# A post-norm decoder layer in three-stage software pipeline: scores of two pairs in one visit, over three banks, and new lists for all engines

## The reference, cut to what matters

```
scores = einsum('bqgre,bkge->bgrqk', q, k) / sqrt(64)      # 16 heads of queries, 8 of keys
probs  = softmax(where(causal_mask, -1e6, scores))
z      = einsum('bgrqk,bkge->bqgre', probs, v)
x = layernorm(x + z @ W_out + b_out)
x = layernorm(x + cross_attention(layernorm_affine(x), ctx, top 5 allowed rows))
x = layernorm(x + (silu(x @ wg.T) * (x @ wu.T)) @ wd.T)
```

## Time and profile before

| | |
|---|---|
| median of 3 runs | 2152.0 us (2150.78 to 2153.03) |
| profiled execution | 2153.04 us, its span 2150.9 us |
| PE / PEld busy | 2081.0 us (97%) / 1857.7 us (86%) |
| DVE / ACT / POOL busy | 1574.1 (73%) / 1328.4 (62%) / 387.2 us (18%) |
| mean granted clock of PE | 0.989 |
| chain that ended last | PE 95% |
| DMA | 38.47 MB, 18 GB/s |

### The profile page before, as it was taken

The page is one execution under the profiler, slowest core; times in us unless marked ns, Lnnn a source line. Parts: engine busy times, 40 slices in busy tenths (PEclk is TensorE's granted clock), DMA queues, the critical chain, the costliest instruction groups (busy, mean ns, idle before and its releaser), DMA issues.

```text
span 2150.9 us, 56003 instructions
## 1 busy us (share of the span) xinstructions
PE 2081.0 (97%) x18368; PEld 1857.7 (86%) x18368; DVE 1574.1 (73%) x5700; ACT 1328.4 (62%) x3990; POOL 387.2 (18%) x630
## 2 busy tenths in 40 slices
PE   4899999999999999999999999999999999999986
PEld 3688988898988998988998988988888988888975
DVE  3477777777777777777777777777777777777764
ACT  4666666666666666666666666666666656666642
POOL 3201111111111111111111112111212111211111
PEclk9899999999999999999999999999999999999998
DMA  4100000000000000000000000000000000000000
GB/s 135 41 14 11 10 18 18 18 18 10 13 13 18 18 18 10 17 9 18 18 18 10 18 8 18 18 18 10 18 8 18 18 18 10 18 8 18 14 6 11
DMA packets 48599, 38.47 MB, mean 18 GB/s; under 512 B 19504, under 2 KB 46512, under 8 KB 48560
## 3 DMA queue, kind: packets, MB, share of 16 engines
q1 hardware_dynamic: 48560, 37.96, 6.3%
HBM read 29.56 MB, written 8.39 MB: 18 GB/s over the span
## 4 chain that ended last, share of the span: by engine, by line
PE 95%; ACT 1%; DVE 1%; DMA 1%; POOL 1%; issue 1%; SPq 0%; POOLq 0%; DVEq 0%; ACTq 0%
PE gen L375 19%; PE gen L377 18%; PE gen L376 18%; PE s_ps L509 10%; PE z_ps L543 6%; PE pt_ps L522 3%; PE gen L470 3%; PE gen L457 3%; PE gen L466 3%; PE z_ps L545 3%; PE pt_ps L523 3%; PE pt_ps L527 3%; PE gen L439 3%; PE gen L481 1%; PE gen L434 1%
## 5 line engine op out<-in xcount | busy, mean ns | idle before, releaser
L679 ACT ACTIVATE SM<-SM,least 128x128 f32<-128x128 f32 (+1 forms) x1024 | 454.1, 449 | 88.4 <-DVE least L975 88.3
L975 DVE CUSTOM_DVE_ANT_0 SM<-s_ps,causal 128x128 f32<-128x128 f32 (+1 forms) x1024 | 311.1, 354 | 157.0 <-PE s_ps L509 99.3
L615 ACT ACTIVATE PT<-pt_ps 128x512 f32<-128x512 f32 (+1 forms) x512 | 245.3, 486 | 153.6 <-PE z_ps L545 91.9
L988 DVE TENSOR_SCALAR SM<-SM,total 128x128 f32<-128x128 f32 (+1 forms) x1024 | 290.2, 347 | 9.1
L509 PE MATMUL s_ps<-KT,QT 64*128 64x128 f32 (+1 forms) x2048 | 237.1, 350 | 6.4 <-ACT KT L615 6.4
L662 ACT ACTIVATE G<-gen 128x256 f32<-128x256 f32 x192 | 73.5, 383 | 245.4 <-PE gen L377 243.3
L1133 POOL TENSOR_TENSOR var<-moments,eps 128x2 f32<-128x2 f32 x96 | 18.7, 195 | 1055.1 <-DVE moments L847 1055.1
L679 ACT ACTIVATION_READ_ACCUMULATOR SM<-SM,least 128x1 f32 x1024 | 197.7, 193 | 0.0
L1157 POOL TENSOR_TENSOR H_lo<-G,H_hi 128x256 fp32r<-128x256 f32 x192 | 141.0, 747 | 293.0 <-ACT H_hi L615 292.9
L509 PEld LDWEIGHTS s_ps<-KT,QT 64*128 64x128 f32 x2048 | 135.4, 188 | 45.4 <-issue 23.4
L543 PE MATMUL z_ps<-PT,Vt 128*64 128x256 f32 x1024 | 170.0, 402 | 2.8 <-ACT PT L615 2.7
(11 more groups left out here) (176 smaller groups left out, 6583.9 us busy)
## 6 DMA issues: line engine op xcount, KB each, us to landing
xT_in<-in_xT SPq DMA_DIRECT2D x32, 256.0 KB, 2.8
x_in<-in_x SPq DMA_DIRECT2D x32, 256.0 KB, 2.8
out<-XN SPq DMA_DIRECT2D x32, 256.0 KB, 2.2
ctx_in<-in_ctxT SPq DMA_DIRECT2D x32, 77.0 KB, 2.4
mask_in<-in_maskT SPq DMA_DIRECT2D x32, 77.0 KB, 2.6
QX<-in_wq SPq DMA_DIRECT2D x1, 512.0 KB, 3.7
QP<-in_wq SPq DMA_DIRECT2D x1, 512.0 KB, 5.5
xwk<-in_xwkv SPq DMA_DIRECT2D x1, 512.0 KB, 5.5
```

The costliest lines, as they stand in the source:

```text
L615: return act.activation(o, i, ACT.Copy)
L679: ins = act.activation(part, part, ACT.Exp, scale=-1.0, bias=least[:, i % 2, n:n + 1], accum_out=total[:, i % 2, n:n + 1])
L975: ins = dve.tensor_tensor_reduce(SM[:, i % 2, at:at + keys], s_ps[h][:, t * P:t * P + keys], causal[:, S - keys:S], -SCALE, -3 * NEG, ALU. ...
L988: ins = dve.tensor_scalar(part, part, total[:, i % 2, n:n + 1], None, ALU.mult)
```

## The change

1. `scores(j)` now makes two pairs, 2j and 2j+1, in one visit: eight matmuls (16 records), four visits an iteration. There are three score banks. The 128-key parts of head 0 and head 1 of both pairs go to banks 0 and 1, as do the 256-key parts of the first pair; both 256-key parts of the second pair go to bank 2. Since head 0 and head 1 run on different array rows, the last matmul waits until the first is through (`s_shared`). DVE's `masked` waits for the whole visit.
2. `BANKS` is 2: two general banks are left.
3. `SM`, `least`, `total` have four places, and `masked(i)` waits for the transposes of pair i-4.
4. The lists of all four engines and `ITEMS` are new. Nothing is computed in another way, and no instruction is added but for the waits.

```diff
-BANKS = 3
+BANKS = 2
+    PLACES = (((0, S), (1, S)), ((0, S + P), (1, S + P))), (((0, 0), (1, 0)), ((2, 0), (2, S)))
-        SM = sb("SM", [P, 2, PAIR])
+        SM = sb("SM", [P, 4, PAIR])
-        s_ps = [bank(f"s_ps{i}") for i in range(2)]
+        s_ps = [bank(f"s_ps{i}") for i in range(3)]
-        s_full = signal("s_full", 2 * NP)
+        s_shared = signal("s_shared", NP // 2)
+        s_full = signal("s_full", NP)
...
-                def scores(i):
+                def scores(j):
...
-                    pe.wait_ge(s_masked.sem, s_masked.at(b, 2 * i))
-                    for t in range(T):
+                    pe.wait_ge(s_masked.sem, s_masked.at(b, 4 * j))
+
+                    def score(n, h, t):
+                        rows = slice(h * E, (h + 1) * E)
                         keys = P * (t + 1)
+                        bank, at = PLACES[t][n][h]
+                        return pe.matmul(s_ps[bank][:, at:at + keys], QT[rows, j % 2, n, t * P:(t + 1) * P],
+                                         KT[rows, j, 0:keys], start=True, stop=True)
+
+                    score(1, 0, 1).then_inc(s_shared.sem, 1)
+                    score(0, 1, 1)
+                    for n in range(2):
                         for h in range(2):
+                            score(n, h, 0)
+                    score(0, 0, 1).then_inc(s_full.sem, 1)
+
+                    pe.wait_ge(s_shared.sem, s_shared.at(b, j + 1))
+                    score(1, 1, 1).then_inc(s_full.sem, 1)
...
-                    dve.wait_ge(pt_full.sem, pt_full.at(b, 2 * i - 2))
-                    dve.wait_ge(s_full.sem, s_full.at(b, 2 * i + h + 1))
+                    dve.wait_ge(pt_full.sem, pt_full.at(b, 2 * i - 6))
+                    dve.wait_ge(s_full.sem, s_full.at(b, 2 * (i // 2) + 2))
```

More of the change, by code:

```diff
@@ L549, in body @@
                 scores(0)
+                fill("oXK")
+                fill("fXOUT")
+                transposed("o", 6)
+                fill("aK1")
                 fill("aQ1")
-                fill("fXOUT")
+                fill("aQ2")
                 transposed("o", 7)
-                fill("oXK")
+                fill("fT3")
+                values("o", 6)
+                values("o", 7)
                 scores(1)
[L555 to L559, removed]
                 transposed("a", 0)
+                fill("fFFN0")
                 fill("oOUT0")
                 fill("oOUT1")
+                fill("fFFN1")
+                fill("fFFN2")
                 transposed("a", 1)
[L564 to L569, removed]
+                fill("aV1")
+                fill("aV0")
                 fill("fFFN3")
[L571 to L574, removed]
+                scores(2)
                 fill("oT10")
                 fill("oT11")
+                values("a", 0)
+                fill("fFFN4")
+                transposed("a", 2)
                 fill("aQ3")
-                scores(5)
+                fill("fFFN5")
+                fill("oXQ1")
                 transposed("a", 3)
-                fill("fFFN4")
-                fill("fFFN5")
                 fill("oXQ0")
-                fill("oXQ1")
-                transposed("a", 4)
-                scores(6)
+                values("a", 1)
+                fill("oSIM10")
+                scores(3)
                 fill("oSIM00")
@@ L588, in body @@
                 values("a", 3)
-                fill("oXV")
-                fill("oSIM10")
-                scores(7)
                 fill("nQ0")
-                transposed("a", 5)
                 fill("nK0")
                 fill("fDOWN1")
+                fill("fDOWN0")
+                transposed("a", 4)
+                fill("oT201")
+                fill("oXV")
                 fill("oT200")
-                fill("fDOWN0")
-                fill("oT201")
+                transposed("a", 5)
+                fill("oT211")
+                fill("oT210")
                 values("a", 4)
+                fill("oXPV0")
                 values("a", 5)
[L601 to L605, removed]
                 fill("oXPV1")
@@ L1085, in body @@
                 probabilities(3)
-                probabilities(4)
+                fill("fFFN4")
                 masked(5, 0)
@@ L1194, in x_low @@
                                        ALU.subtract).then_inc(xT_low.sem, 1)
+                x_bias()
                 deviation_2()
+                gated_low(0)
                 context_low()
-                x_bias()
                 both_deviations()
-                gated_low(0)
                 gated_low(1)
```

188 lines of the change are left out of this document (91 added, 97 removed), and 6 rows, old and new, of the table ITEMS.

## The result

The changed kernel takes 2111.9 us (median of four runs, 2110.16 to 2114.27), the kernel before beside it 2151.39 us: a ratio of 0.9815, 95% interval 0.9802 to 0.9827. The profiled execution took 2110.16 us, 42.9 less than that of before.

What follows compares the result with a forecast made beforehand. PE's own list was taken as the bound: -1.60 + 0.05 + 0.12 + 0.10 = -1.33 us an iteration, -39 over 29, -2 for iterations 1 and 31, -41 from 2153.0: 2112, median 2111 us; range 2095 to 2142.

Steps and rivals of the forecast that it cites:

- The bound: Steady iterations: PE never waits, busy for all of 1863.90 us, so the time is PE's own list.
- Changes of shape: PE's list: 14 switches of array tiling an iteration for 23, at 0.16 to 0.20 us each, saving 1.6 us.
- The wait on s_shared: Last matmul of a scores visit: release just in time, 0; blocks behind it with thin lead, 0.05 us an iteration together.
- The bound of 0.15 a visit on a late release: Scores visits: upper end if the s_shared release comes wholly on top, 0.15 x 4 = 0.6 us an iteration.
- Rival D: Scores visits: last pair not side by side, 0.43 us added to each, gain gone, 2148 to 2156 us; chance 0.06.
- Two banks, DVE beside POOL: PE waiting on two general banks, 0.12 us an iteration; DVE slowed by POOL, late for fFFN3, 0.10.
- rivals B and C: B: thin covers cost, 2120 to 2143 us, chance 0.20. C: slower through waits for two banks, 2178, chance 0.11.
- thin covers: Bank fills with little work ahead: oSIM10 late by 0.05 to 0.1 us, fFFN4 0 to 0.1, oT11 in time by 0.24.
- part 4: DVE, POOL and four places: later masked costs PE nothing, DVE beside POOL may delay fFFN3; 0.1 us an iteration taken.
- the weights': 0: Iteration 0: its length belongs to the late weights, so no change in time.
- -1 was expected: Iteration 1: mostly PE's too, 49.29 of 53.50 us busy; iterations 1 and 31 were put at -2 us together.
- the 5 allowed: Tail after 2060 or so: chains set the time and one more pair ends in iteration r; 0, within 5 us either way.

Runs made afterwards that it cites:

- e5_split: The kernel before with two blocks of PE's list taken apart, 27 changes of shape for 23: 64.98 us a steady iteration, 2172.2 us whole (one run).
- e6_place: The changed kernel with SM places 2 and 3 and total behind the last tile, all else at the addresses of before: 62.75 us an iteration, 2104.5 us whole.
- e4_late: The changed kernel with a visit's first and seventh matmul exchanged, so the awaited one stands directly ahead of the s_shared wait: 65.94 us an iteration, 2203.9 us (one run).
- e11_slots: The changed kernel, tiles behind SM at the old addresses, with all late weights placed anew in ACT's list: iteration 0 49.9 us, whole 2101.8 us.
- e13_kq: The kernel before with late(4) ahead of probs_out(a, 2, 0), copies of aK1 and aQ2 ahead of late(3): iteration 0 57.8 us, whole 2152.8 us.

## Why the prediction was right, point by point

**The bound.** PE's own list bounds the kernel, in both. The 36.1 us of the steady stretch came off PE's busy time, as read from the earlier trace rows.

**Changes of shape.** Nine fewer at 0.18 us, -1.60 an iteration. e5_split measured 0.18 for each of four added. With the tiles at the addresses of before (e6_place) the changed kernel's iteration is 1.52 us shorter than before, 0.17 for each of nine. This step carried the forecast, and it was shown by itself.

**The wait on s_shared.** Held to cost nothing itself, and 0.05 in the blocks behind it. The visit's last pass starts 1.20 us after its first and no weight load waits for PE, so the first is right, and no block behind it starts late, so the 0.05 did not come. The bound of 0.15 a visit on a late release was too low: e4_late shows 0.33 for the release and what hangs on it, and 0.42 more for passes that lose their neighbours. Rival D is excluded for this kernel by the 1.20.

**Two banks, DVE beside POOL.** Held to cost 0.12 and 0.10. By the starts and the gaps between weight loads (above) both are nothing in the steady stretch, and with them rivals B and C. Of the thin covers oSIM10 was worked out to be late by 0.05 to 0.1, fFFN4 by 0 to 0.1, and oT11 to be in time by 0.24; all held. oSIM10 started 1.02 us after the last start of oXQ0, so the chain worked out at 1.06 takes no longer than that. In iterations 1, 2 and 31 it did come late, by 0.24, 0.15 and 0.15 us.

**What the sum lacked.** The terms make -1.33, the measurement is -1.24. Without the 0.27 for waits that did not come the sum would have been -1.60, and 0.36 was missing on the other side. Of it, 0.28 is the place of the tiles: the prediction took a larger `SM` for free (its part 4 has no term for it), and e6_place takes exactly this back. The remaining 0.08 has no experiment of its own: it is what 0.17 in place of 0.18 a change makes, and the XOUT products run at 0.12 us a matmul in the changed kernel with either placement, some 0.16 us an iteration more than in before, so that something else must have become a little cheaper. So two mistakes of about equal size cancelled, 0.27 for waits and 0.36 unseen. That the sum lies within 0.1 of the measurement is luck; that it has the right size without them is the term of the changes of shape.

**The ends.** Iteration 0 was put down as "the weights': 0", and it gave 7.8 us, more than a sixth of the gain (5.3 to 7.8 with the same lists and the tiles elsewhere). The step that failed is that sentence: PE was busy 38.59 of 58.50 us there, so it was waiting, and every list that touches it was new. By the rows, PE's busy time there fell by 5.6 us, from 38.59 to 32.99, and its idle time by 2.2, from 19.9 to 17.7. Two parts of the 5.6 can be named. There are 234 matmul records in place of 248, and 1028 in place of 1015 from iteration 31 on, since pair 6 is now finished an iteration later: work that moved from one end to the other. And the mean granted clock was 0.83 in place of 0.80. How much each gave was not measured. As to the waits, the late weights are not a fixed length of their own; they and attention take turns in ACT's list: e11_slots halved a wait of 8.35 us by their position alone, and e13_kq only moved one. Which feature of the new lists took the rest off is not settled: single edits to the kernel before gave 0.7 us and 0.6 us at most, and four places 1.2, which is no more than e5_split shows without such an edit. The changed kernel's lists with two places in `SM` were not tried.

Iteration 1 gave +0.8 where -1 was expected. Its rows show two things that no experiment took apart. PE is idle for 4.95 us in place of 4.21, with these as the longest waits, the first of them for the masking of the visit before, which the change made one for two pairs:

```profile
PE s_ps L513 <- DVE least L983: 2.1, 1, 2.1
PE gen L470 <- DVE SX L915: 2.0, 1, 2.0
```

And the granted clock is 0.97 in place of 1.00. The second wait ends at 118.90, and then PE has the lower level of 1.2 GHz from 120.0 to 123.4 (the 0.50 in this row of the columns above), which costs 1.7 us at most:

```profile
120.00:123.40 3.40, 3.40 (x15) 2.74 (x13) 3.06 (x14) 1.62 (x4) 0.00 (x0) 0.50 0.00 0
```

In the tail, +1.7 us, inside the 5 allowed, with the 13 records that moved there:

```profile
PE gen L485 <- DVE X L860: 5.6, 2, 4.0
PE gen L379 <- POOL H_lo L1165: 2.7, 1, 2.7
PE gen L438 <- DVE XN L1025: 1.9, 1, 1.9
```

These are the changed kernel's longest waits of the tail, and the same kinds as in the tail of before; the tail's difference was not taken apart further.

**The total.** -36.1 against -39, and -6.4 at the ends against -2: -42.5 against -41. The total is closer than its parts.

## What to carry to other kernels

Where PE never waits, count how often its list changes the array's shape: each change cost 0.18 us here, inside the busy time. A semaphore that PE gives itself cost 0.33 us here with nothing between, and 0.42 more because two passes lost the neighbours that they ran beside; with six matmuls between it cost nothing. To see such a wait, ask for the waits of the weight loads. And when a buffer grows, run a kernel with the buffer grown and nothing else: here that alone was +0.45% of an iteration, and the changed kernel got 0.28 us of it back when the new part went behind all other tiles.

## What the runs showed of the hardware

The pace of a stream of 256-column matmuls depends on where tiles lie in SBUF: 0.113 or 0.119 us each for the same DOWN product, and shifts of 32, 64 and 6208 bytes each moved the iteration, by 0.16 to 0.29 us. The change is in PE's pace, not in a wait, so neither idle time nor the view of waits shows it. PE waiting for its own semaphore shows in the waits of PEld, 0.46 us each in e4_late, and not in those of PE.
